# Windowed attention: one copy taken ahead of a masked score, one projection chunk and its rotation sooner, reciprocals behind rotations

## The chip, the cores and the metric

One Trainium2 chip, one of its cores. The time is that of the whole kernel on the device, in microseconds (us). An execution is one launch; the median of three launches is given. One further launch was profiled.

## What is computed

The program is a chain of four stages over 16 sequences of 512 tokens with 256 features: windowed attention, an int8 layer, a linear attention and a feed-forward layer, each followed by a layer norm. The change touches only the first stage, which the kernel does completely before the other three:

```
qkv = x @ w_qkv                                   # 16 heads of 64
q, k = l2norm(q) * q_scale, l2norm(k) * k_scale
bq = rotary(q * 8);  bk, bv = look_around(k, v)   # windows of 128; previous, own and next window
sim = where(mask, -big, einsum('bwid,bwjd->bwij', bq, bk))
out = einsum('bwij,bwjd->bwid', softmax(sim), bv)
x = layernorm(x + out @ w_out)
```

## The kernel before

All matrices are float32; projections are made of three products of high and low parts. The heads go in pairs, 8 pairs (p = 0 to 7) for each of 16 sequences, so 128 pairs. A sequence has four windows w = 0 to 3. Windows 0 and 3 have 256 keys, windows 1 and 2 have 384. In the code i is the number of a window counted over all pairs, n that of a pair, h the head in the pair (0 or 1).

Each engine runs its own program, written out by hand: for each pair two halves, u = 0 and u = 1 (`pe_half`, `act_half`, `dve_half`, `pool_half`). Work is done some way ahead. Half (p, u = 1) of pair n does three things side by side:

- it finishes windows 2 and 3 of pair n: TensorE transposes their softmax weights (`pe_transpose_weights`), ScalarE copies those of head 0 out of bank tp (`act_evacuate_weights`), VectorE those of head 1 (`dve_evacuate_weights`);
- it scores windows 0 and 1 of pair n+1: `pe_scores`, then on VectorE `dve_mask_max` (norm factor, mask, row maximum; the profile calls it CUSTOM_DVE_ANT_0), on ScalarE `act_exp` with the row sum, on VectorE `dve_reciprocals`, on GpSimd `pool_softmax` (scales the rows of both heads);
- it projects chunks 2 and 3 (of 128 tokens) of pair n+2: `pe_project` into banks pj, `act_project` on ScalarE (copy of v, square of q and k), `dve_rotate` on VectorE (two products, L510 and L511), `pool_rotate` on GpSimd (their sum).

Half (p+1, u = 0) then begins. On TensorE it is: `pe_values` of pair n (L331, weights times values, into bank qk), `pe_scores` of windows 2 and 3 of pair n+1 (L303), `pe_q_transpose` of pair n+2 (L278, into bank qk), and further on the transposes of windows 0 and 1 (L322), chunks 0 and 1 of the next projection (L267) and `pe_k_transpose` (L285). `pe_q_transpose` waits for `rot_pool`, that is for GpSimd's sum of chunk 3, and for `ot_act`, ScalarE's copy of the values' result (L445).

On GpSimd the order at this place is: softmax of window 0, softmax of window 1, rotation of chunk 2 (end of half u = 1), rotation of chunk 3, key norm (start of half u = 0). Its queue is in order, as are those of ScalarE and VectorE. `pool_softmax` waits for `rc_dve`, the reciprocal.

On VectorE half u = 1 ends: copy of window 2, `dve_mask_max` of window 1 head 1, reciprocal of window 0, copy of window 3, reciprocal of window 1, rotation of chunk 2. Half u = 0 starts: rotation of chunk 3, `dve_norms`, then the masked scores. On ScalarE half u = 1 ends with the exponential of window 1 head 1 and the projection of chunk 2, and half u = 0 starts with the projection of chunk 3.

A window is called spare when it is window 3 of a pair with p not 0 or 6. The transposes of head 1 of a spare window go to bank qk; those of other windows go to a score bank, sc.

Each sequence's layer norm is done while the next sequence runs: statistics of tokens in `dve_stats` (second half at the start of half (1,0)), `norm.rstd` on GpSimd at the end of half (1,0) (a power, L84, and a product, L86), `norm.apply` on ScalarE in half (2,0) ahead of `act_o_evacuate`.

The functions that the change touches:

Of the kernel before, what the change touches and what calls it, by code (L numbers as in the profile page):

```python
# [18 lines left out]
PAIRS = HEADS // 2  # L19
PW = 2 * DH  # L20
WS = 128
NW = S // WS
# [77 lines left out]
def run_attention(nc, io, mem, psum):  # L100
    SC, TP, PJ, QK = (psum['sc'], psum['tp'], psum['pj'], psum['qk'])

    def spare(i):
        pair, w = divmod(i, NW)
        return w == 3 and pair % PAIRS not in (0, 6)
# [14 lines left out]
    def span(w):  # L120
        lo, hi = (max(0, w - 1), min(NW - 1, w + 1))
        return lo, hi, (hi - lo + 1) * WS
# [200 lines left out]
        last.then_inc(g['t_pe'], 1)  # L323

    def pe_values(e, n, p):
        e.wait_ge(g['pt_act'], NW * n + NW)
        e.wait_ge(g['pt_dve'], NW * n + NW)
        for k in range(NW):
            lo, hi, width = span(k)
            for h in range(2):  # L330
                last = e.matmul(QK[rows(h), lo * WS:(hi + 1) * WS], v[p % 4][:, k, rows(h)], pt_keys(h, k),  # L331
                    start=k == 0, stop=k == NW - 1, skip_group_check=True)
        last.then_inc(g['pv_pe'], 1)
# [81 lines left out]
    def act_project(e, m, p, t):  # L415
        e.wait_ge(g['pj_pe'], TT * m + t + 1)
        e.activation(v[p % 4][:, t, :], PJ[t % 2][:, 2 * PW:3 * PW], ACT.Copy)
        e.activation(sq[:, t, :], PJ[t % 2][:, 0:2 * PW], ACT.Square).then_inc(g['sq_act'], 1)  # L418
# [11 lines left out]
    def act_exp(e, i, w, h):  # L430
        lo, hi, width = span(w)
        e.wait_ge(g['sm_dve'], 2 * i + h + 1)
        e.activation(ex[h][w][:, 0:width], sm[h][w % 2][:, 0:width], ACT.Exp, bias=nm[:, w, h:h + 1], scale=-1.0,  # L433
            accum_out=rs[:, w, h:h + 1]).then_inc(g['e_act'], 1)
# [16 lines left out]
    def act_half(e, at):  # L451
        n, p, u, i, w = (at.pair, at.p, at.u, at.window, at.w)
        ahead, next_i, next_w = (at.has_next(), at.next_window, at.next_w)
        if u == 0:
            if at.has_pair(1):
                act_project(e, n + 1, (p + 1) % PAIRS, 3)
            if at.at(2, 0) and not at.first:
                norm.apply(e, at.b - 1, mem['res'])
            if at.has_pair(-1):
                act_o_evacuate(e, n - 1, (p - 1) % PAIRS)  # L460
            if at.has_pair(1):
                act_norms(e, n + 1, (p + 1) % 2)
            if ahead:
                act_exp(e, next_i, next_w, 0)
            act_evacuate_weights(e, i, w)
            if ahead:
                act_exp(e, next_i, next_w, 1)
                act_exp(e, next_i + 1, next_w + 1, 0)
            if at.has_pair(2):
                act_project(e, n + 2, (p + 2) % PAIRS, w)  # L470
            if at.has_pair(1):
                act_k_evacuate(e, n + 1, (p + 1) % 2)
            act_evacuate_weights(e, i + 1, w + 1)
            if ahead:
                act_exp(e, next_i + 1, next_w + 1, 1)
        else:
            if at.has_pair(2):
                act_project(e, n + 2, (p + 2) % PAIRS, 1)
            if not at.last:
                if at.at(5, 1):  # L480
                    act_x(e, at.b + 1, 0)
                if at.at(6, 1):
                    act_x(e, at.b + 1, 1)
            act_evacuate_weights(e, i, w)
            if ahead:
                act_exp(e, next_i, next_w, 0)
                act_exp(e, next_i, next_w, 1)
                act_exp(e, next_i + 1, next_w + 1, 0)
            act_evacuate_weights(e, i + 1, w + 1)
            if ahead:  # L490
                act_exp(e, next_i + 1, next_w + 1, 1)
            if at.has_pair(2):
                act_project(e, n + 2, (p + 2) % PAIRS, w)
        if at.first and (at.at(0, 0) or at.at(2, 0)):
            act_weights_high(e, 3 + p // 2)
        if w1_piece(at) is not None:
            act_next_weights(e, w1_piece(at))
# [6 lines left out]
    def dve_rotate(e, m, t):  # L504
        e.wait_ge(g['sq_act'], TT * m + t + 1)
        if due(TT * m + t - 1):
            e.wait_ge(g['rot_pool'], TT * m + t - 1)
        heads = 'p (k h d) -> p k h d'
        qk = PJ[t % 2][:, 0:2 * PW].rearrange(heads, k=2, h=2)
        e.tensor_tensor(ra[:, t % 2, :].rearrange(heads, k=2, h=2), qk, rotary(t, 0), ALU.mult)  # L510
        last = e.tensor_tensor(rb[:, t % 2, :].rearrange(heads, k=2, h=2), qk, rotary(t, 1), ALU.mult)  # L511
        last.then_inc(g['rot_dve'], 1)

    def dve_norms(e, m):
        e.wait_ge(g['sq_act'], TT * m + TT)
        e.tensor_reduce(ss[:, 0, :], sq[:, :, :].rearrange('p t (h d) -> p (t h) d', d=DH), AX.X,
            ALU.add).then_inc(g['raw_dve'], 1)
        e.wait_ge(g['raw_dve'], m + 1)
        e.tensor_scalar(ss[:, 1, :], ss[:, 0, :], NORM_FLOOR ** 2, None, ALU.max).then_inc(g['ss_dve'], 1)
# [25 lines left out]
    def dve_residual(e, seq, k):  # L545
        e.wait_ge(g['op_pe'], 2 * seq + k + 1)
        if k == 0:
            e.wait_ge(g['x_keep'], 16 * (seq + 1))
            if due(seq):
                e.wait_ge(g['y_out'], 16 * seq)  # L550
        e.tensor_tensor(halves(mem['res'], k), QK[:, :], halves(mem['xres'], k), ALU.add).then_inc(g['op_dve'], 1)  # L551

    def dve_stats(e, seq, k):
        e.wait_ge(g['op_dve'], 2 * seq + k + 1)
        norm.stats(e, seq, mem['res'], (2 * k, 2 * k + 1))
# [7 lines left out]
    def dve_half(e, at):  # L563
        n, p, u, i, w = (at.pair, at.p, at.u, at.window, at.w)
        ahead, next_i, next_w, par = (at.has_next(), at.next_window, at.next_w, at.next_par)
        out = at.at(0, 1) and not at.first
        if u == 0 and at.has_pair(1):
            dve_rotate(e, n + 1, 3)
            dve_norms(e, n + 1)
        if u == 1 and at.has_pair(2):  # L570
            dve_rotate(e, n + 2, 1)
        if not at.first:
            if at.at(1, 0):
                dve_stats(e, at.b - 1, 1)
        if ahead:
            dve_mask_max(e, next_i, par, next_w, 0)
            dve_mask_max(e, next_i, par, next_w, 1)
        if not at.last:
            if at.at(5, 1):
                dve_x(e, at.b + 1, 0)  # L580
            if at.at(6, 1):
                dve_x(e, at.b + 1, 1)
        if u == 0 and at.has_pair(1):
            dve_q_evacuate(e, n + 1, (p + 1) % 2)
        if ahead:
            dve_mask_max(e, next_i + 1, par, next_w + 1, 0)
        if out:
            dve_residual(e, at.b - 1, 0)
        dve_evacuate_weights(e, i, w)
        if ahead:  # L590
            dve_mask_max(e, next_i + 1, par, next_w + 1, 1)
            dve_reciprocals(e, next_i, next_w)
        if out:
            dve_stats(e, at.b - 1, 0)
            dve_residual(e, at.b - 1, 1)
        dve_evacuate_weights(e, i + 1, w + 1)
        if ahead:
            dve_reciprocals(e, next_i + 1, next_w + 1)
        if at.has_pair(2):
            dve_rotate(e, n + 2, w)  # L600
        if at.first and (at.at(0, 1) or at.at(2, 1)):
            dve_weights_low(e, 3 + p // 2)
        if not at.first:
            for t, step in enumerate(((2, 1), (3, 0), (3, 1), (4, 0))):
                if at.at(*step):
                    dve_amax(e, at.b - 1, t)
# [27 lines left out]
    def pool_half(e, at):  # L634
        n, p, u, i, w = (at.pair, at.p, at.u, at.window, at.w)
        if u == 0 and at.has_pair(1):
            pool_rotate(e, n + 1, (p + 1) % 2, 3)
            pool_k_norm(e, n + 1, (p + 1) % 2)
        if u == 1 and at.has_pair(2):
            pool_rotate(e, n + 2, p % 2, 1)  # L640
        if at.has_next():
            pool_softmax(e, at.next_window, at.next_w)
            pool_softmax(e, at.next_window + 1, at.next_w + 1)
        if at.has_pair(2):
            pool_rotate(e, n + 2, p % 2, w)
        if at.at(1, 0) and not at.first:
            norm.rstd(e, at.b - 1)
        if at.first and (at.at(0, 1) or at.at(2, 1)):
            pool_weights_low(e, 3 + p // 2)
        if w1_piece(at) is not None:  # L650
            pool_next_weights(e, w1_piece(at))
# [1280 lines left out]
```

## Time and profile before

| | us |
|---|---|
| median of three launches (3098.9 to 3100.77) | 3100.35 |
| the profiled launch | 3097.64 |
| its span, first to last instruction | 3095.8 |
| TensorE busy | 2941.9 (95%) |
| VectorE busy | 2357.9 (76%) |
| ScalarE busy | 2162.1 (70%) |
| GpSimd busy | 1662.0 (54%) |

Busy times are of the whole span. Matmuls overlap their predecessors, so TensorE's busy share counts some waiting too: start times tell more than the share. In rows of the timeline the first number is the start in us from the start of the span, the second the length of the group; the bracket at the end gives the idle time before the group and what ended it. PE is TensorE, DVE VectorE, ACT ScalarE, POOL GpSimd.

### The profile page before, as it was taken

How to read it: one execution, taken by the hardware profiler on the slowest of the kernel's cores; microseconds unless marked ns; L12 is line 12 of the kernel's file. 1: busy time of each engine (PE TensorE's matmuls, PEld its weight loads, DVE VectorE, ACT ScalarE, POOL GpSimd, SP SyncE). 2: the span in 40 equal slices, each digit the busy share in tenths (PEclk: the TensorE clock that was granted, in tenths of full speed). 3: DMA queues.
4: the chain of work that ended last, by engine and by line, in shares of the span. 5: the costliest groups of instructions: out<-in, count | busy, mean ns of one | idle time of the engine just before them, and what ended most of it. 6: DMA issues, size and time to landing. Idle time of an engine off the chain costs nothing. (4 is left out here: it accounts for less than half of the span.)

```text
span 3095.8 us, 60269 instructions
## 1 busy us (share of the span) xinstructions
PE 2941.9 (95%) x20143; PEld 2332.4 (75%) x20143; DVE 2357.9 (76%) x6845; ACT 2162.1 (70%) x5670; POOL 1662.0 (54%) x2226
## 2 busy tenths in 40 slices
PE   7999999999999999999999996799999999999996
PEld 5777777777777777777777774578888888888885
DVE  6877877877877877877877875787777777777775
ACT  5666766766766766766766764577888888888884
POOL 5655655655655655655655654344555555555555
PEclk9999999999999999999999998899999999999998
DMA  2000000000000000000000002100000000000000
GB/s 84 8 15 22 8 15 22 8 15 22 8 15 17 13 15 15 15 15 15 15 15 15 8 21 64 47 15 8 15 15 15 21 20 16 15 15 15 8 15 21
DMA packets 51218, 57.50 MB, mean 19 GB/s; under 512 B 3008, under 2 KB 48592, under 8 KB 50912
## 3 DMA queue, kind: packets, MB, share of 16 engines
q1 hardware_dynamic: 47904, 50.67, 5.1%
q8 instruction: 164, 2.69, 0.4%
q10 hardware_dynamic: 3008, 2.98, 0.3%
q14 instruction: 142, 1.16, 0.1%
HBM read 36.86 MB, written 16.78 MB: 17 GB/s over the span
## 5 line engine op out<-in xcount | busy, mean ns | idle before, releaser
L627 POOL TENSOR_SCALAR a_ex<-a_ex,a_rc 128x384 f32<-128x384 f32 (+1 forms) x1024 | 533.8, 536 | 691.4 <-DVE a_rc L538 691.2
L433 ACT ACTIVATE a_ex<-a_sm,a_nm 128x384 f32<-128x384 f32 (+1 forms) x1024 | 572.0, 560 | 72.5 <-DVE a_nm L531 61.2
L531 DVE CUSTOM_DVE_ANT_0 a_sm<-sc,a_mask,a_rn 128x384 f32<-128x384 f32 (+1 forms) x1024 | 529.7, 543 | 6.3 <-PE sc L303 6.3
L439 ACT ACTIVATE a_pt<-tp 128x256 f32<-128x256 f32 (+1 forms) x512 | 220.1, 430 | 290.5 <-PE tp L322 290.5
L267 PE MATMUL pj<-a_whi,a_xhi 128*128 128x384 f32 x1024 | 390.3, 381 | 8.8 <-DVE a_wlo L187 5.8
L1695 POOL TENSOR_TENSOR b_alo<-b_ring,b_ahi 128x512 fp32r<-128x512 f32 x128 | 169.6, 1325 | 411.7 <-DVE b_ring L1524 388.0
L611 POOL TENSOR_TENSOR a_qr<-a_ra,a_rb 128x256 f32<-128x256 f32 x512 | 370.5, 739 | 11.2 <-DVE a_rb L511 8.4
L267 PE MATMUL pj<-a_whi,a_xlo 128*128 128x384 f32 x1024 | 347.4, 339 | 0.0
L267 PE MATMUL pj<-a_wlo,a_xhi 128*128 128x384 f32 x1024 | 346.3, 338 | 0.0
L331 PE MATMUL qk<-a_pt,a_v 128*64 128x384 f32 (+1 forms) x2048 | 303.9, 437 | 29.0 <-DVE a_pt L543 26.8
L303 PE MATMUL sc<-a_kT,a_qT 64*64 64x256 f32 (+1 forms) x4096 | 307.6, 415 | 1.6 <-DVE a_nm L531 0.9
L331 PEld LDWEIGHTS qk<-a_pt,a_v 128*64 128x64 f32 x2048 | 158.3, 136 | 156.3 <-issue 63.9
L543 DVE COPY a_pt<-sc 128x384 f32<-128x384 f32 (+1 forms) x416 | 209.7, 504 | 72.0 <-PE sc L322 65.9
L510 DVE TENSOR_TENSOR a_ra<-pj,a_rot 128x256 f32<-128x256 f32 x512 | 214.3, 419 | 39.9 <-ACT a_sq L418 39.7
L322 PE MATMUL tp<-s_ident,a_ex 128*128 128x128 f32 x1280 | 228.9, 277 | 3.2 <-ACT a_pt L439 1.3
L342 PE MATMUL qk<-a_wo,a_ot 128*128 128x256 f32 x1024 | 228.0, 381 | 1.5 <-DVE a_res L551 0.8
L303 PEld LDWEIGHTS sc<-a_kT,a_qT 64*64 64x64 f32 x4096 | 131.5, 132 | 129.0 <-issue 80.7
L342 PEld LDWEIGHTS qk<-a_wo,a_ot 128*128 128x128 f32 x1024 | 192.0, 190 | 34.5 <-issue 7.4
L1491 DVE SCALAR_TENSOR_TENSOR b_ring<-k,b_one_bk,b_ring 128x512 f32<-128x512 f32 x128 | 95.8, 749 | 153.1 <-ACT b_ring L1355 149.8
L511 DVE TENSOR_TENSOR a_rb<-pj,a_rot 128x256 f32<-128x256 f32 x512 | 211.6, 413 | 0.0
L267 PEld LDWEIGHTS pj<-a_whi,a_xhi 128*128 128x128 f32 x1024 | 194.5, 190 | 12.5 <-issue 6.3
L322 PE MATMUL sc<-s_ident,a_ex 128*128 128x128 f32 x1088 | 192.4, 278 | 8.3 <-DVE a_nm L531 4.9
(234 smaller groups left out, 7988.7 us busy)
## 6 DMA issues: line engine op xcount, KB each, us to landing
a_xres<-x SPq DMA_DIRECT2D x16, 512.0 KB, 3.8
y<-a_res SPq DMA_DIRECT2D x16, 512.0 KB, 2.9
b_y<-y SPq DMA_DIRECT2D x16, 512.0 KB, 3.8
a_xin<-x SPq DMA_DIRECT2D x15, 512.0 KB, 3.8
out<-b_y SPq DMA_DIRECT2D x15, 512.0 KB, 2.9
a_xin<-wqkv SPq DMA_DIRECT2D x8, 256.0 KB, 2.7
a_ot<-wqkv ACTq DMA_DIRECT2D x3, 384.0 KB, 9.8
a_stage<-wqkv SPq DMA_DIRECT2D x3, 384.0 KB, 12.3
```

The source lines that it names most:

```text
L267: last = e.matmul(PJ[t % 2][:, 0:3 * PW], a[:, c, t * P:(t + 1) * P], w[:, c, p * 3 * PW:(p + 1) * 3 * PW], start=c == 0 and k == 0, stop= ...
L303: last = e.matmul(SC[j][h][a * DH:(a + 1) * DH, first:first + wide], qT[par][rows(h), queries:queries + DH], kT[par][rows(h), lo * WS + fi ...
L322: last = e.transpose(tp_bank(h, i)[:, k * P:(k + 1) * P], ex[h][w][:, k * P:(k + 1) * P], ident[:, :])
L331: last = e.matmul(QK[rows(h), lo * WS:(hi + 1) * WS], v[p % 4][:, k, rows(h)], pt_keys(h, k), start=k == 0, stop=k == NW - 1, skip_group_c ...
L342: last = e.matmul(QK[:, t * DIM:(t + 1) * DIM], ot[:, c, (2 * k + t) * P:(2 * k + t + 1) * P], wo[:, c, :], start=c == 0, stop=c == HC - 1)
L433: e.activation(ex[h][w][:, 0:width], sm[h][w % 2][:, 0:width], ACT.Exp, bias=nm[:, w, h:h + 1], scale=-1.0, accum_out=rs[:, w, h:h + 1]).t ...
L439: e.activation(pt_window(0, w), blocks(TP, w), ACT.Copy).then_inc(g['pt_act'], 1)
L510: e.tensor_tensor(ra[:, t % 2, :].rearrange(heads, k=2, h=2), qk, rotary(t, 0), ALU.mult)
L511: last = e.tensor_tensor(rb[:, t % 2, :].rearrange(heads, k=2, h=2), qk, rotary(t, 1), ALU.mult)
L531: e.tensor_tensor_reduce(out=sm[h][w % 2][:, 0:width], in0=SC[w % 2][h][:, 0:width], in1=mem['mask'][:, off:off + width], scale=rn[:, par, ...
L611: e.tensor_tensor(qr[par][:, t, :].rearrange(half, h=4, s=2), ra[:, t % 2, :].rearrange(half, h=4, s=2), rb[:, t % 2, :].rearrange(half, h ...
L627: e.tensor_scalar(row, row, 0.0, rc[:, w, h:h + 1], ALU.add, ALU.mult).then_inc(g['exn_pool'], 1)
```

## The change

In `pe_values` the wait for all four windows' copies is split: key windows 0 and 1 start after three windows' copies (where window 3 is spare, VectorE's copies of all four are still awaited), key windows 2 and 3 after all four. In halves u = 1 ScalarE projects chunk 2 right after the first exponential. In halves u = 1 with a spare window, VectorE copies window 3 and rotates chunk 2 ahead of the last `dve_mask_max`, and the reciprocal of window 1 moves into the next half, behind the rotation of chunk 3. In halves u = 0 the last reciprocal goes behind the rotation of chunk 0. The second part of `dve_stats` moves from the start of half (1,0) to its end, and `norm.rstd` from half (1,0) to half (1,1).

```diff
     def pe_values(e, n, p):
-        e.wait_ge(g['pt_act'], NW * n + NW)
-        e.wait_ge(g['pt_dve'], NW * n + NW)
         for k in range(NW):
             lo, hi, width = span(k)
+            if k in (0, 2):
+                e.wait_ge(g['pt_act'], NW * n + NW - 1 + k // 2)
+                e.wait_ge(g['pt_dve'], NW * n + (NW if k or spare(NW * n + NW - 1) else NW - 1))
...
             act_evacuate_weights(e, i, w)
             if ahead:
                 act_exp(e, next_i, next_w, 0)
+            if at.has_pair(2):
+                act_project(e, n + 2, (p + 2) % PAIRS, w)
+            if ahead:
                 act_exp(e, next_i, next_w, 1)
                 act_exp(e, next_i + 1, next_w + 1, 0)
             act_evacuate_weights(e, i + 1, w + 1)
             if ahead:
                 act_exp(e, next_i + 1, next_w + 1, 1)
-            if at.has_pair(2):
-                act_project(e, n + 2, (p + 2) % PAIRS, w)
...
         if u == 0 and at.has_pair(1):
             dve_rotate(e, n + 1, 3)
+        if u == 0 and i and spare(i - 1):
+            dve_reciprocals(e, i + 1, w + 1)
+        if u == 0 and at.has_pair(1):
             dve_norms(e, n + 1)
         if u == 1 and at.has_pair(2):
             dve_rotate(e, n + 2, 1)
-        if not at.first:
-            if at.at(1, 0):
-                dve_stats(e, at.b - 1, 1)
...
         dve_evacuate_weights(e, i, w)
-        if ahead:
+        if ahead and u == 1 and spare(i + 1):
+            dve_evacuate_weights(e, i + 1, w + 1)
+            if at.has_pair(2):
+                dve_rotate(e, n + 2, w)
             dve_mask_max(e, next_i + 1, par, next_w + 1, 1)
             dve_reciprocals(e, next_i, next_w)
-        if out:
-            dve_stats(e, at.b - 1, 0)
-            dve_residual(e, at.b - 1, 1)
-        dve_evacuate_weights(e, i + 1, w + 1)
-        if ahead:
-            dve_reciprocals(e, next_i + 1, next_w + 1)
-        if at.has_pair(2):
-            dve_rotate(e, n + 2, w)
+        else:
+            if ahead:
+                dve_mask_max(e, next_i + 1, par, next_w + 1, 1)
+                dve_reciprocals(e, next_i, next_w)
+            if out:
+                dve_stats(e, at.b - 1, 0)
+                dve_residual(e, at.b - 1, 1)
+            dve_evacuate_weights(e, i + 1, w + 1)
+            if u == 0 and at.has_pair(2):
+                dve_rotate(e, n + 2, w)
+            if ahead:
+                dve_reciprocals(e, next_i + 1, next_w + 1)
+            if u == 1 and at.has_pair(2):
+                dve_rotate(e, n + 2, w)
+        if at.at(1, 0) and not at.first:
+            dve_stats(e, at.b - 1, 1)
...
-        if at.at(1, 0) and not at.first:
+        if at.at(1, 1) and not at.first:
             norm.rstd(e, at.b - 1)
```

## Rows read from the trace of the kernel before

**Rows 1.** Timeline of PE, half (7,1) and the next: start, length, engine, line.
```profile
957.19 1.20 PE L303 MATMUL sc<-a_kT,a_qT 64*64 64x256 f32 x16
...
959.76 0.49 PE L322 MATMUL sc<-s_ident,a_ex 128*128 128x128 f32 x3
...
961.92 2.38 PE L331 MATMUL qk<-a_pt,a_v 128*64 128x256 f32 x16 [0.19 <-DVE a_pt L543]
964.23 1.20 PE L303 MATMUL sc<-a_kT,a_qT 64*64 64x320 f32 x16
965.36 0.66 PE L278 MATMUL qk<-s_ident,a_qr 128*128 128x128 f32 x4
...
969.61 0.66 PE L303 MATMUL sc<-a_kT,a_qT 64*64 64x256 f32 x8
```

**Rows 2.** Timeline of DVE, same stretch.
```profile
960.29 0.56 DVE L543 COPY a_pt<-sc 128x384 f32<-128x384 f32 x1 [0.21 <-PE sc L322]
960.76 0.61 DVE L531 CUSTOM_DVE_ANT_0 a_sm<-sc,a_mask,a_rn 128x384 f32<-128x384 f32 x1
...
961.29 0.16 DVE L538 RECIPROCAL a_rc<-a_rs 128x2 f32<-128x2 f32 x1
961.37 0.41 DVE L543 COPY a_pt<-qk 128x256 f32<-128x256 f32 x1
...
962.59 0.42 DVE L510 TENSOR_TENSOR a_ra<-pj,a_rot 128x256 f32<-128x256 f32 x1 [0.27 <-ACT a_sq L418]
...
963.26 0.41 DVE L510 TENSOR_TENSOR a_ra<-pj,a_rot 128x256 f32<-128x256 f32 x1
```

**Rows 3.** Timeline of ACT, same stretch.
```profile
961.41 0.61 ACT L433 ACTIVATE a_ex<-a_sm,a_nm 128x384 f32<-128x384 f32 x1 [0.17 <-DVE a_nm L531]
...
962.18 0.37 ACT L418 ACTIVATE a_sq<-pj 128x256 f32<-128x256 f32 x1
```

**Rows 4.** Timeline of POOL, same stretch.
```profile
961.56 2.07 POOL L627 TENSOR_SCALAR a_ex<-a_ex,a_rc 128x256 f32<-128x256 f32 x4 [1.72 <-DVE a_rc L538]
963.59 1.42 POOL L611 TENSOR_TENSOR a_qr<-a_ra,a_rb 128x256 f32<-128x256 f32 x2
```

**Rows 5.** Timeline of PE, half (4,1) and the next half's query transposes.
```profile
917.85 1.20 PE L303 MATMUL sc<-a_kT,a_qT 64*64 64x256 f32 x16
...
926.47 0.66 PE L278 MATMUL qk<-s_ident,a_qr 128*128 128x128 f32 x4
```

**Rows 6.** Timeline of PE, half (1,1) and the next half's query transposes.
```profile
879.50 1.20 PE L303 MATMUL sc<-a_kT,a_qT 64*64 64x256 f32 x16
...
888.03 0.63 PE L278 MATMUL qk<-s_ident,a_qr 128*128 128x128 f32 x4 [0.15 <-ACT a_ot L445]
```

**Rows 7.** Timeline of POOL, end of half (1,0) and start of (1,1).
```profile
881.85 1.02 POOL L84 TENSOR_TENSOR a_ln_rs<-a_ln_ve,a_half 128x4 f32<-128x4 f32 x1
...
883.10 0.74 POOL L611 TENSOR_TENSOR a_qr<-a_ra,a_rb 128x256 f32<-128x256 f32 x1
```

**Rows 8.** Timeline of ACT, half (2,0).
```profile
885.32 2.08 ACT L92 ACTIVATE a_res<-a_res,a_ln_shift,a_ln_rs 128x256 f32<-128x256 f32 x4
```

**Rows 9.** Timeline of PE in the first sequence: the query transposes that waited.
```profile
33.46 0.66 PE L278 MATMUL qk<-s_ident,a_qr 128*128 128x128 f32 x4 [2.32 <-POOL a_qr L611]
...
39.28 0.93 PE L303 MATMUL sc<-a_kT,a_qT 64*64 64x256 f32 x12
...
50.32 0.66 PE L278 MATMUL qk<-s_ident,a_qr 128*128 128x128 f32 x4 [2.01 <-POOL a_qr L611]
...
80.02 0.66 PE L278 MATMUL qk<-s_ident,a_qr 128*128 128x128 f32 x4 [2.10 <-POOL a_qr L611]
```

**Rows 10.** Windows: length, busy us (count) of each engine, PEclk, DMA share, GB/s.
```profile
34.10:37.50 3.40, 3.40 (x16) 3.30 (x14) 2.50 (x9) 2.79 (x10) 1.05 (x1) 0.50 0.02 5
51.10:54.50 3.40, 3.40 (x15) 3.30 (x15) 1.91 (x7) 2.19 (x8) 0.36 (x1) 0.51 0.00 0
81.50:85.00 3.50, 3.50 (x33) 2.95 (x35) 2.50 (x10) 3.29 (x12) 1.62 (x4) 1.00 0.00 0
```

## Prediction

> **What bounds the kernel now.** I read the page first: TensorE is the fullest engine, and the stage that the change touches is the first of four. Then I read the timeline of TensorE over one sequence by start times, because overlapping matmuls hide waits in a busy share. Nearly every step from one matmul to the next is as short as it can be for its shapes. The exceptions are small: in most pairs the values (L331) start late, waiting for VectorE's copy of window 3; the bracket says 0.19 us in the pair shown [rows 1]. So TensorE bounds the stage, and the other engines matter only where a result that it awaits comes late. The timelines of the three others over the same stretch tell how much room each result has. The one with least room is the query transposes (L278): TensorE reaches them at 965.36 [rows 1], and GpSimd's sums of chunks 2 and 3 end at 963.59 + 1.42 = 965.01 [rows 4]. That is 0.35 us of slack, at the end of a queue that starts with the softmax scaling of windows 0 and 1.
>
> **The chain to the query transposes, before.** Last masked score 960.76, its exponential 961.41 [rows 2, 3], GpSimd busy without a gap from 961.56 to 965.01, with the softmax of both windows first and both rotations after [rows 4]. I call the start of the half's scores T0 = 957.19; the transposes come at T0 + 8.17, the next half's scores at 969.61, 4.25 us after them [rows 1].
>
> **The same chain after, step by step.** VectorE's queue now holds the copies of windows 2 and 3, the rotation of chunk 2, and only then the last masked score.
> 1. Copy of window 2: it waits for TensorE's transposes at present (idle 0.21) and starts at 960.29; they aren't earlier now. It takes 0.47 to the next start [rows 2].
> 2. Copy of window 3 (narrow): 0.41 long [rows 2], of which some 0.06 overlaps the next instruction, as every VectorE group here starts a little before its predecessor's end; 0.35. At 961.11 window 3 is copied. TensorE could start the values sooner by the bracket's 0.19; I take 0.25, since overlapping starts hide a little of a wait, so 961.67 instead of 961.92, and this copy doesn't hold it up any more. That is the gain, and it is right.
> 3. Rotation of chunk 2: 963.26 - 962.59 = 0.67 [rows 2]. Its input is ready, since ScalarE now projects chunk 2 two exponentials sooner. Ends 961.78.
> 4. Last masked score starts 961.78 instead of 960.76: 1.02 us later.
> 5. Its exponential 0.65 after the score's start (960.76 to 961.41), as before [rows 2, 3]: 962.43. ScalarE then goes straight on to chunk 3 of the projection. Before, chunk 2 stood between; its square starts 0.77 after the exponential [rows 3]. I use that 0.77 for chunk 3's: 963.20.
> 6. Rotation of chunk 3 starts 0.41 after the square (962.18 to 962.59) [rows 2, 3]: 963.61. It takes 0.67: 964.28.
> 7. Only now comes the reciprocal of window 1, which was free to run since about 963.1. GpSimd starts 0.27 after a reciprocal (961.29 to 961.56) [rows 2, 4]: 964.55.
> 8. Softmax of window 1: all four scalings take 963.59 - 961.56 = 2.03 [rows 4], by width 384/640 of that, 1.22: 965.77.
> 9. Rotations of chunks 2 and 3 stand behind it in GpSimd's queue, though chunk 2's products have been there for 4 us: 1.42 [rows 4], 967.19; transposes at 967.24, T0 + 10.05.
>
> So the query transposes come 10.05 - 8.17 = 1.88 us later, although TensorE is through with values and scores 0.25 sooner. What follows them is TensorE's own work, 4.25 us to the next T0, and the next half u = 1 starts from the same state, because step 1 hangs on TensorE. The delay repeats in each pair.
>
> **The sum over a sequence.** Halves like (7,1): pairs 7 and 2, and I take pair 5 (which also splits the next input) as the same: 3 x 1.88 = 5.64. Pairs 3 and 4 lose 8.62 already (917.85 to 926.47 [rows 5]), a wait that goes with the earlier rotation of chunk 0: 2 x (10.05 - 8.62) = 2.86. Pair 6 keeps VectorE's order, but there ScalarE now waits, with two exponentials and a copy queued behind it, for a projection that TensorE does only after window 3's first transposes; both reciprocals and GpSimd hang on these exponentials. No row prices it; it lies between 0 (slack hides it) and 1.88 (the chain above), and I take 1.0, nearer the middle.
>
> Pair 1 is the dear one. The rstd moves from GpSimd's idle stretch to the place between rotations of chunks 2 and 3, and takes 883.10 - 881.85 = 1.25 [rows 7]. Worse, `norm.apply` on ScalarE waits for it, and behind it are queued the copy of the values' result and the norms. Rotation 2 ends at T0 + 10.05 - 0.05 - 0.71 = T0 + 9.29; rstd until 10.54; apply at 10.59; from the apply's start to the transposes it is 888.03 - 885.32 = 2.71 as now [rows 6, 8]: T0 + 13.30. Before: 888.03 - 879.50 = 8.53 [rows 6]. That is 4.77. Moving `dve_stats` gives TensorE something back in half (1,0), whose key transposes wait for VectorE, and costs most of it again at the next masked scores: no row separates these; between a gain of 0.8 and a loss of 0.6 I take 0.2 gained. Pair 1: 4.6. Pair 0 gets 0 (a gain of at most 0.2).
>
> Per sequence 5.64 + 2.86 + 1.0 + 4.6 = 14.1. Fourteen full ones: 197. The first has no norm to do (pair 1 as pair 7, 11.4), the last nothing after pair 5 (11.2). Together 220 us.
>
> The split wait of `pe_values` itself costs nothing: key windows 2 and 3 come half of 2.3 us after the first (961.92 to 964.23 [rows 1]), and ScalarE's copy, one projection later than before, is there by then. If it were not, TensorE would wait some tenths, in time that it now waits anyway at the transposes.
>
> **The clock.** TensorE will stand still from the end of the scores, 963.98 + 1.20 = 965.18, to 967.24: 2.0 us in each of 80 pairs and over 5 us in 15 (pair 1). The trace has three such stalls at the same instruction: 2.32, 2.01 and 2.10 us [rows 9]. After two of them the granted clock was 0.50 (the 1.2 GHz level), after the third 1.00 [rows 10]. The first of them took 39.28 - 33.46 = 5.82 from transposes to next scores [rows 9] against 4.25 [rows 1]: 1.57 us for a fall. I take a fall after every second of the 80, between none and all: 63 us, and one in each pair 1: 24 us.
>
> The Trainium skill, page "TensorE: Matmul & The Clock Gate", section "HAM oscillation — how this bites in real kernels", describes how a loop that waits between bursts of matmuls finds the clock throttled again each time. Taken to the letter for every pair here it gives 149 us where I take 87; the two stalls of three agree with it, the third speaks against "each time".
>
> **Sum.** The profiled launch took 3097.64, the median 3100.35, 2.7 more. 220 + 87 = 307; 3097.64 + 307 + 2.7 = 3407, which I round to 3405 us.
>
> **The rivals.**
> - *Stalls without the clock* (chance 0.17): the delay is as above but the clock stays at 1.00, as after the third stall; 3100 + 220 = 3320. For it: full work on both sides of the stall.
> - *A fall after every stall* (0.12), the skill's rule taken to the letter: 3320 + 95 x 1.57 = 3469.
> - *Only the sequence boundary hurts* (0.07): the rotations turn out to leave room in ordinary pairs, and pair 1's rstd and apply alone are late: 3100 + 15 x 4.6 = 3169. Against it: 0.35 us of slack and 2.2 us more in the chain.
> - *Faster* (0.08): GpSimd's chain stays hidden, so that TensorE keeps what it gains at the values, 0.19 to 0.25 in a pair (128 x 0.25 = 32 us), and some waits of masked scores and key transposes on top, 20 us: about 3050. It decides itself at step 7: window 1's reciprocal would have to run by some 962.7, 1.6 us before my 964.28, for instance if ScalarE had chunk 3 done before the last exponential. The order of its queue speaks against that.
> - *No change* (0.03): the gains and pair 1's loss cancel, which needs ordinary pairs to lose nothing.
>
> My forecast, with falls after part of the stalls, has 0.53. Faster and slower are counted from 0.2%, about what measurement of this kernel can tell from no change: faster 0.08, same 0.03, slower 0.89. The range goes from somewhat under the case without the clock (3290) to the case of all falls (3470).
>
> **What would show it.** In the trace after: TensorE's L278 idle some 2 us with GpSimd's L611 named, in pairs 1 to 5 and 7, over 5 us once a sequence with ScalarE's L445 named; no idle at L331 before the values; GpSimd idle between the softmaxes of window 0 and 1; stretches of clock 0.50 all through the first stage; the other stages unchanged. I am wrong if the reciprocal of window 1 doesn't end up behind a rotation that waits for ScalarE, or if TensorE does other work during that time.

## The result

The changed kernel takes 3375.5 us (median of 6 launches, 3373.4 to 3379.4) against 3099.6 for the kernel before in the same session: ratio 1.089, 95% interval 1.0876 to 1.0904. The forecast was 3405 us, slower. (In two of the experiments below one launch of four took far longer, 5817 and 10133 us, for a reason that nothing here shows; their times are medians of the other three.) The profiled launch has a span of 3377.6 us against 3095.8, 281.8 more. The last matmul of the attention stage ends at 2192.4 instead of 1914.2, so 278 of these 282 us are in that stage.

The page of the kernel after (span, and busy time, share and number of instructions by engine) has TensorE 89% busy instead of 95%, with the same 20143 matmuls:

```profile
span 3377.6 us, 60397 instructions
PE 3012.0 (89%) x20143; PEld 2398.0 (71%) x20143; DVE 2364.3 (70%) x6845; ACT 2194.2 (65%) x5670; POOL 1661.0 (49%) x2226
```

TensorE's waits, from 200 to 1800 us (us in total, times, longest):

```profile
PE qk L278 <- POOL a_qr L624: 124.6, 72, 2.0
PE qk L278 <- ACT a_ot L446: 63.8, 12, 5.3
PE sc L322 <- DVE a_nm L533: 7.2, 11, 0.7
```

Before, in the same stretch:

```profile
PE qk L331 <- DVE a_pt L543: 22.8, 82, 0.5
...
PE qk L278 <- ACT a_ot L445: 1.5, 10, 0.2
```

The largest wait, that of the values (L331) for VectorE's copy, is gone: where rows 1 have a bracket of 0.19 at the values, there is none now. In its place stand 72 waits of the query transposes (L278) for GpSimd's rotation and, once a sequence, one of 5.3 us for ScalarE's copy of the values' result.

Half (7,1) after, TensorE; it answers to [rows 1]:

```profile
1092.71 1.20 PE L303 MATMUL sc<-a_kT,a_qT 64*64 64x256 f32 x16
...
1095.28 0.49 PE L322 MATMUL sc<-s_ident,a_ex 128*128 128x128 f32 x3
...
1097.19 2.38 PE L332 MATMUL qk<-a_pt,a_v 128*64 128x256 f32 x16
1099.49 1.20 PE L303 MATMUL sc<-a_kT,a_qT 64*64 64x320 f32 x16
1102.62 0.66 PE L278 MATMUL qk<-s_ident,a_qr 128*128 128x128 f32 x4 [1.92 <-POOL a_qr L624]
...
1106.88 1.20 PE L303 MATMUL sc<-a_kT,a_qT 64*64 64x256 f32 x16
```

With T0 = 1092.71 the values start at T0 + 4.48 (before 4.73) and the transposes at T0 + 9.91 (before 8.17). The next scores follow 4.26 later (before 4.25). VectorE, which answers to [rows 2]:

```profile
1095.81 0.56 DVE L545 COPY a_pt<-sc 128x384 f32<-128x384 f32 x1 [0.24 <-PE sc L322]
1096.28 0.41 DVE L545 COPY a_pt<-qk 128x256 f32<-128x256 f32 x1
1096.61 0.42 DVE L512 TENSOR_TENSOR a_ra<-pj,a_rot 128x256 f32<-128x256 f32 x1
...
1097.27 0.61 DVE L533 CUSTOM_DVE_ANT_0 a_sm<-sc,a_mask,a_rn 128x384 f32<-128x384 f32 x1
...
1097.81 0.16 DVE L540 RECIPROCAL a_rc<-a_rs 128x2 f32<-128x2 f32 x1
1099.10 0.42 DVE L512 TENSOR_TENSOR a_ra<-pj,a_rot 128x256 f32<-128x256 f32 x1 [1.13 <-ACT a_sq L419]
...
1099.78 0.16 DVE L540 RECIPROCAL a_rc<-a_rs 128x2 f32<-128x2 f32 x1
```

ScalarE [rows 3] and GpSimd [rows 4]:

```profile
1097.01 0.38 ACT L440 ACTIVATE a_pt<-tp 128x256 f32<-128x256 f32 x1
1097.93 0.62 ACT L434 ACTIVATE a_ex<-a_sm,a_nm 128x384 f32<-128x384 f32 x1 [0.54 <-DVE a_nm L533]
...
1098.70 0.37 ACT L419 ACTIVATE a_sq<-pj 128x256 f32<-128x256 f32 x1
```

```profile
1098.07 0.94 POOL L640 TENSOR_SCALAR a_ex<-a_ex,a_rc 128x256 f32<-128x256 f32 x2 [2.45 <-DVE a_rc L540]
1100.03 1.15 POOL L640 TENSOR_SCALAR a_ex<-a_ex,a_rc 128x384 f32<-128x384 f32 x2 [1.02 <-DVE a_rc L540]
1101.15 1.42 POOL L624 TENSOR_TENSOR a_qr<-a_ra,a_rb 128x256 f32<-128x256 f32 x2
```

Read in this order it is the chain of the forecast: the score starts at 1097.27, behind a copy and a rotation; exponential 1097.93; square of chunk 3 1098.70; its rotation 1099.10, for which VectorE sat idle 1.13 us, while the reciprocal stood behind it; reciprocal 1099.78; softmax of window 1 at 1100.03; and both rotations on GpSimd only at 1101.15, though the products of chunk 2 were complete by 1097.4. GpSimd idles 2.45 and 1.02 us ahead of the two softmaxes. The values start at 1097.19 while ScalarE's copy of window 3 (L440) runs until 1097.39: so their gain needs the split wait as well as VectorE's sooner copy. The mended kernel with VectorE's old order, below, has the split wait without the sooner copy, and its values start at T0 + 4.73 again; no run has the sooner copy alone.

The sequence boundary, half (1,1) and (2,0), on TensorE [rows 6], GpSimd [rows 7] and ScalarE [rows 8]:

```profile
863.22 1.20 PE L303 MATMUL sc<-a_kT,a_qT 64*64 64x256 f32 x16
...
866.61 0.52 PE L322 MATMUL sc<-s_ident,a_ex 128*128 128x128 f32 x3 [0.66 <-DVE a_nm L533]
...
877.37 1.09 PE L278 MATMUL qk<-s_ident,a_qr 128*128 128x128 f32 x4 [5.30 <-ACT a_ot L446]
```

```profile
872.65 0.73 POOL L624 TENSOR_TENSOR a_qr<-a_ra,a_rb 128x256 f32<-128x256 f32 x1
873.34 1.02 POOL L84 TENSOR_TENSOR a_ln_rs<-a_ln_ve,a_half 128x4 f32<-128x4 f32 x1
874.43 0.20 POOL L86 TENSOR_TENSOR a_ln_shift<-a_ln_minus,a_ln_rs 128x4 f32<-128x4 f32 x1
874.59 0.72 POOL L624 TENSOR_TENSOR a_qr<-a_ra,a_rb 128x256 f32<-128x256 f32 x1
```

```profile
874.67 2.08 ACT L92 ACTIVATE a_res<-a_res,a_ln_shift,a_ln_rs 128x256 f32<-128x256 f32 x4 [4.09 <-POOL a_ln_shift L86]
876.65 0.58 ACT L446 ACTIVATE a_ot<-qk 128x512 f32<-128x512 f32 x1
```

ScalarE stands 4.09 us in front of the apply. Its copy of the values' result is queued behind, and the transposes behind that: T0 + 14.15, before T0 + 8.53. At the bracket of 0.66, ahead of the transposes of softmax weights, TensorE pays for the statistics, which VectorE now does ahead of this half's masked scores.

The same two distances for all pairs, medians over the sequences (15 in pairs 6 and 7, 16 in the others), each from the start times in the timeline of TensorE (those at full clock where there are any, so that only pair 1 after has the clock's cost in it; "mended" is an experiment below):

| pair | T0 to query transposes: before | after | mended | then to the next T0: before | after | mended |
|---|---|---|---|---|---|---|
| 0 | 21.94 | 21.78 | 21.78 | 5.22 | 4.26 | 5.21 |
| 1 | 8.52 | 14.15 | 8.29 | 4.22 | 6.52 | 4.23 |
| 2 | 8.16 | 9.91 | 7.91 | 4.40 | 4.27 | 4.26 |
| 3 | 8.62 | 9.90 | 7.91 | 4.41 | 4.26 | 4.26 |
| 4 | 8.62 | 9.90 | 7.91 | 4.25 | 4.27 | 4.26 |
| 5 | 8.73 | 10.40 | 8.34 | 4.25 | 4.25 | 4.26 |
| 6 | 9.23 | 9.94 | 9.15 | 4.26 | 4.26 | 4.25 |
| 7 | 8.17 | 9.90 | 7.91 | 4.26 | 4.26 | 4.26 |

The granted clock of a stretch behind a stall of 1.92 us in another sequence's pair 7, and behind one of 5.3 us (columns as in [rows 10]):

```profile
967.60:971.00 3.40, 3.40 (x15) 3.31 (x15) 1.81 (x7) 2.34 (x8) 0.39 (x2) 0.50 0.00 0
875.40:878.80 3.40, 1.43 (x7) 1.46 (x8) 0.30 (x1) 2.75 (x8) 1.05 (x1) 0.51 0.33 112
875.40:882.20 6.80, 4.83 (x20) 4.76 (x21) 1.99 (x7) 4.85 (x16) 1.05 (x1) 0.50 0.23 77
```

I call such a stretch at 0.50 a fall of the clock. Where it fell in an ordinary pair (2 to 5 and 7), the way from the transposes to the next scores took 5.83 us instead of 4.26; in the pair 1 shown the low clock lasted until 882.2, and the way took 6.52. It fell after 4 of 16 stalls in pair 2, none in pair 3, 9 of 16 in pair 4, 8 of 16 in pair 5, 8 of 15 in pair 7 and all 16 in pair 1. Between the first and the last sequence the falls of pairs 4 and 7 come in every second sequence, and those of pair 5 in the others.

These stalls aren't all of one length. In the first sequence that of pair 1 is 1.92 us and that of pair 2 3.83, in the last those of pairs 4 and 5 are 3.7. Sorted by length, the clock fell after 27 of 77 stalls of 1.9 to 2.0 us, after all 3 of 3.7 to 3.8 and all 15 of 5.3.

### The profile page after: what moved, and what is told of

Its sections match the earlier page's. It is cut to its first block and busy times, and to the rows that moved or that the text cites. A ratio compares the mean times of both kernels' runs of the same rounds, so it can differ in the third digit from the quotient of the medians.

```text
span 3377.6 us, 60397 instructions
## 1 busy us (share of the span) xinstructions
PE 3012.0 (89%) x20143; PEld 2398.0 (71%) x20143; DVE 2364.3 (70%) x6845; ACT 2194.2 (65%) x5670; POOL 1661.0 (49%) x2226
## 5 line engine op out<-in xcount | busy, mean ns | idle before, releaser
L440 ACT ACTIVATE a_pt<-tp 128x256 f32<-128x256 f32 (+1 forms) x512 | 223.2, 436 | 386.4 <-PE tp L322 385.6
L267 PE MATMUL pj<-a_whi,a_xhi 128*128 128x384 f32 x1024 | 405.3, 396 | 8.3 <-DVE a_wlo L187 5.0
L267 PE MATMUL pj<-a_whi,a_xlo 128*128 128x384 f32 x1024 | 361.6, 353 | 0.0
L267 PE MATMUL pj<-a_wlo,a_xhi 128*128 128x384 f32 x1024 | 360.1, 352 | 0.0
L278 PE MATMUL qk<-s_ident,a_qr 128*128 128x128 f32 x512 | 91.3, 305 | 255.2 <-POOL a_qr L624 175.5
L278 PEld LDWEIGHTS qk<-s_ident,a_qr 128*128 128x128 f32 x512 | 58.7, 150 | 311.5 <-POOL a_qr L624 219.6
L322 PE MATMUL tp<-s_ident,a_ex 128*128 128x128 f32 x1280 | 244.2, 292 | 8.4 <-ACT a_pt L440 7.8
L332 PEld LDWEIGHTS qk<-a_pt,a_v 128*64 128x64 f32 x2048 | 137.1, 137 | 143.1 <-issue 120.7
L322 PE MATMUL sc<-s_ident,a_ex 128*128 128x128 f32 x1088 | 204.7, 292 | 9.9 <-DVE a_nm L533 9.8
```

The source lines that it names most:

```text
L267: last = e.matmul(PJ[t % 2][:, 0:3 * PW], a[:, c, t * P:(t + 1) * P], w[:, c, p * 3 * PW:(p + 1) * 3 * PW], start=c == 0 and k == 0, stop= ...
L322: last = e.transpose(tp_bank(h, i)[:, k * P:(k + 1) * P], ex[h][w][:, k * P:(k + 1) * P], ident[:, :])
L440: e.activation(pt_window(0, w), blocks(TP, w), ACT.Copy).then_inc(g['pt_act'], 1)
```

## The experiments

Each was timed against the kernel before on the same chip. The theory: the query transposes are the end of one serial chain (last masked score, exponential, square of chunk 3, rotation of chunk 3, reciprocal, softmax of window 1, two rotations on GpSimd), and at the sequence boundary of a longer one through rstd and apply; stalls cost a second time through the clock.

**Reciprocal ahead of the rotation of chunk 3.** On the changed kernel:

```diff
         if u == 0 and at.has_pair(1):
-            dve_rotate(e, n + 1, 3)
         if u == 0 and i and spare(i - 1):
             dve_reciprocals(e, i + 1, w + 1)
         if u == 0 and at.has_pair(1):
+            dve_rotate(e, n + 1, 3)
             dve_norms(e, n + 1)
```

> The changed kernel with one edit: window 1's deferred reciprocal stands ahead of the rotation of chunk 3, not behind it. Theory (GpSimd's queue holds both rotations behind the softmax of window 1, which waits for this reciprocal): the reciprocal runs when the last exponential is done instead of about 1.1 us later, so the query transposes come about 1.0 us sooner after T0 (8.9 instead of 9.9), the stall before them shrinks from 1.92 to about 0.95 us in each of 80 pairs and by 1.0 in pair 1, and the clock stops falling in ordinary pairs (about 32 falls of 1.57 us): 3375 - 95 - 50 = 3230 us. Rival (the rotation of chunk 2 ahead of the last masked score alone makes the stall, the reciprocal's place is covered): query transposes stay at T0 + 9.9 and the time at 3375 us.

Measured: 3240.8 us (ratio 1.0453, 1.0438 to 1.0469), transposes at T0 + 8.85. In ordinary pairs the clock falls three times only, once in the first sequence and twice in the last, after stalls of 3.4, 2.2 and 2.1 us, and after none of the stalls of at most 1.0 us.

```profile
PE qk L278 <- POOL a_qr L623: 66.8, 78, 1.0
PE qk L278 <- ACT a_ot L446: 51.1, 12, 4.3
```

(the same waits, same stretch). The longest stalls went from 2.0 to 1.0 and from 5.3 to 4.3: the reciprocal's place is 1.05 us of the chain and was not covered. 135 us of the 276 hang on the order of two neighbouring instructions; summed over the pairs of the two traces, some 98 are the sooner transposes and 37 the clock. The rival is out.

**Last masked score ahead of the rotation of chunk 2**, reciprocal still deferred. On the changed kernel:

```diff
             dve_evacuate_weights(e, i + 1, w + 1)
-            if at.has_pair(2):
-                dve_rotate(e, n + 2, w)
             dve_mask_max(e, next_i + 1, par, next_w + 1, 1)
             dve_reciprocals(e, next_i, next_w)
+            if at.has_pair(2):
+                dve_rotate(e, n + 2, w)
```

> The changed kernel with the rotation of chunk 2 behind the last masked score and the first reciprocal again; the copy of window 3 stays ahead of the score, the second reciprocal stays deferred. Theory (the chain from the last masked score is serial down to the query transposes, so each part of the delay counts by its own length): the transposes come 0.67 us sooner, at T0 + 9.23 instead of 9.90; the stall of 1.25 us no longer brings the clock down. 3375 - 95 x 0.67 - 50 = 3262 us. Rival (the deferral alone makes the stall and the rotation's place is covered): T0 + 9.9 and 3375 us.

Measured: 3270.1 us (1.0545, 1.053 to 1.0559), transposes at T0 + 9.25. The rotation counts by its 0.65 us, so the two parts of the delay add up, as in a serial chain: with the copy's 0.33 they make 2.03, and the chain's end moved from T0 + 7.82 (before) to T0 + 9.86, by 2.04.

**Layer norm at its old places.** On the changed kernel:

```diff
+        if not at.first:
+            if at.at(1, 0):
+                dve_stats(e, at.b - 1, 1)
         if ahead:
             dve_mask_max(e, next_i, par, next_w, 0)
...
-        if at.at(1, 0) and not at.first:
-            dve_stats(e, at.b - 1, 1)
...
-        if at.at(1, 1) and not at.first:
+        if at.at(1, 0) and not at.first:
             norm.rstd(e, at.b - 1)
```

> The changed kernel with the layer norm's statistics and rstd at their old places (start and end of half (1,0)). Theory (rstd between the two rotations delays the apply and all that stands behind it on ScalarE): the stalls of 5.3 us in pair 1 become stalls of about 1.9 us, 15 falls of the clock go with them, and the key transposes of half (1,0) wait 0.9 us again: 15 x (3.4 + 2.3 - 0.9) = 72 us less, 3303 us. Rival (pair 1's long stall hides other late work, so that little comes back): 3355 us or more.

Measured: 3299.5 us (1.0643, 1.0626 to 1.0661), 76 us less than the changed kernel; pair 1 at T0 + 9.89, like its neighbours, and the key transposes of half (1,0) wait again (T0 of the next half 5.21 after the transposes, not 4.26). The ordinary stalls are as long as in the changed kernel (1.91 us, in the last sequence 3.7 in pairs 4 and 5), but the clock now falls after all 31 in pairs 4 and 7 and after none in pair 3: the length of such a stall alone doesn't decide it.

**Only the layer norm moved.** On the kernel before:

```diff
-        if not at.first:
-            if at.at(1, 0):
-                dve_stats(e, at.b - 1, 1)
...
+        if at.at(1, 0) and not at.first:
+            dve_stats(e, at.b - 1, 1)
...
-        if at.at(1, 0) and not at.first:
+        if at.at(1, 1) and not at.first:
             norm.rstd(e, at.b - 1)
```

> The kernel before with only the statistics and rstd moved as in the change. Theory: pair 1 alone loses. Rstd's 1.25 us and the apply behind it put the query transposes of half (2,0) about 2.7 us later, half (1,0) gives back about 0.9 and half (1,1) loses most of that at its first masked scores, and the clock falls in each of these 15 stalls of over 3 us: 15 x (2.6 + 1.57) = 63 us more, 3163 us. Rival (the move is harmless by itself and hurts only behind the delayed rotations): 3100 us, or some 13 us under it, by the 0.9 us that the key transposes no longer wait.

Measured: 3155.8 us (1.0182, 1.016 to 1.0205; launches of 3151 to 3164). The waits of the values are as before; new is

```profile
PE qk L278 <- ACT a_ot L445: 37.4, 13, 2.9
```

The longest is 2.9 us, not 5.3: here rstd has a shorter chain in front of it. The clock fell after 12 of the 15. This part alone costs some 56 us; undone in the changed kernel it gave 76.

**The stall filled.** On the changed kernel, transposes that nothing reads:

```diff
         if u == 0:
+            if at.has_pair(1) and n and spare(NW * n - 1):
+                for k in range(17):
+                    e.transpose(TP[:, (k % 4) * P:(k % 4 + 1) * P], ident[:, :], ident[:, :])
             if at.has_pair(1):
                 pe_q_transpose(e, n, n + 1, (p + 1) % 2)
```

> The changed kernel with 17 further transposes of the identity matrix into the free bank tp, ahead of each query transposes that follow a pair with a spare window. They take 17 x 0.109 = 1.85 us of TensorE and fall in its stall; nothing reads them. Theory (the stall costs a second time through the clock): the query transposes stay at T0 + 9.9, but the half-clock stretches behind the stalls of 1.92 us are gone, 32 x 1.57 = 50 us less, 3325 us; those behind pair 1's long stalls may stay. Rival (the slower sections aren't caused by the stall but by something else in these pairs): as many half-clock stretches as before and 3375 us.

Measured: 3314.5 us (1.0685, 1.0665 to 1.0706), 61 us less with 1615 matmuls more. The filler lies in the stall:

```profile
911.41 1.20 PE L303 MATMUL sc<-a_kT,a_qT 64*64 64x320 f32 x16
912.54 2.08 PE L368 MATMUL tp<-s_ident 128*128 128x128 f32 x17
914.60 0.66 PE L278 MATMUL qk<-s_ident,a_qr 128*128 128x128 f32 x4
```

The transposes stay at T0 + 9.91 and the clock no longer falls in pairs 2 to 7; it still falls in 13 of the 15 pairs 1 in which a stall, now of 3.3 us, is left. So the falls come from the stalls. 29 falls in pairs 2 to 7 at 1.57 us are 46 us; in pair 1 the ways to the next T0 are 15 us shorter in sum (where the clock fell, 5.81 instead of 6.52). Together that is the measured 61.

**GpSimd rotates ahead of the softmax of window 1.** On the changed kernel:

```diff
         if u == 0 and at.has_pair(1):
             pool_rotate(e, n + 1, (p + 1) % 2, 3)
+        if u == 0 and i:
+            pool_softmax(e, i + 1, 1)
+        if u == 0 and at.has_pair(1):
             pool_k_norm(e, n + 1, (p + 1) % 2)
...
         if at.has_next():
             pool_softmax(e, at.next_window, at.next_w)
-            pool_softmax(e, at.next_window + 1, at.next_w + 1)
+            if u == 0:
+                pool_softmax(e, at.next_window + 1, at.next_w + 1)
```

> The changed kernel with another order on GpSimd: both rotations ahead of the softmax of window 1, which moves into the next half behind the rotation of chunk 3. VectorE's order, the deferred reciprocal included, stays. Theory (the reciprocal hurts only because two rotations are queued behind its softmax): the query transposes of ordinary pairs come at T0 + 7.95, where TensorE itself arrives, and no stall is left there; in pair 1 rstd and apply still stand ahead, T0 + 11.1, with a fall of the clock. 3375 - 156 - 50 - 46 = about 3120 us, between 3100 and 3130. Rival (VectorE's products of chunk 3 are themselves too late, behind ScalarE's last exponential): a stall of 1 us or more is left in ordinary pairs and the time stays over 3200 us.

Measured: 3177.0 us (1.0245, 1.0227 to 1.0264). The transposes come at T0 + 8.01, as expected, but the time is 47 us over the expected range. Two things that I hadn't counted: from the transposes to the next T0 it takes 4.63 instead of 4.26 us, because the key transposes now wait for VectorE's copy of the query transposes, which is queued behind the rotation of chunk 3, the norms and two masked scores; and in pair 1 the clock fell after 13 of 15 stalls of 3.2 us, and the way from the transposes to the next T0 took 7.05 us there, 1.25 us more than one fall costs elsewhere.

**The same with rstd sooner**, behind the rotation of chunk 1 in half (1,1):

```diff
         if u == 1 and at.has_pair(2):
             pool_rotate(e, n + 2, p % 2, 1)
+        if at.at(1, 1) and not at.first:
+            norm.rstd(e, at.b - 1)
...
-        if at.at(1, 1) and not at.first:
-            norm.rstd(e, at.b - 1)
```

> As the kernel with the new GpSimd order, and rstd at the start of half (1,1), behind the rotation of chunk 1, where GpSimd waits for the first reciprocal anyway. Theory: nothing of the delay is left, TensorE keeps what the change gives it at the values (0.25 us in a pair, more in pairs 3 and 4) and at the key transposes of half (1,0) (0.9 us a sequence): about 2.5 to 3.5 us a sequence less than the kernel before, 3050 to 3060 us. Rival (the late softmax of window 1 now holds up its transposes, or the norms the key transposes): a new wait of TensorE at L322 or L285 and 3100 us or more.

Measured: 3107.3 us (1.0030, 1.0018 to 1.0042): the first theory's gain isn't there, the rival is right. TensorE's waits:

```profile
PE qk L285 <- DVE a_qT L525: 14.9, 84, 0.2
PE qk L278 <- ACT a_ot L446: 14.5, 13, 1.1
PE sc L322 <- DVE a_nm L533: 8.5, 13, 0.7
```

The 84 small waits at the key transposes are the new bound. The bracket shows at most 0.2 us; by start times each costs 0.37. Pair 1 loses too: T0 + 9.95, before 8.52, of which half (1,0) gives back 0.96.

**The kernel before with the GpSimd order alone** (the two edits of `pool_half` shown above, nothing else).

> The kernel before with the new GpSimd order alone. Theory: there the query transposes wait for nothing of GpSimd's and TensorE bounds the pair, so a sooner rotation brings nothing: 3100 us, within 0.3%. Rival (GpSimd's queue was a bound already before): 10 us or more less.

Measured: 3103.8 us (1.0013, 1.0004 to 1.0022), a tenth of a per cent slower. Nothing to gain there: the query transposes of pairs 2, 3, 4 and 7 come when they came before (T0 + 8.17 and 8.62), since they didn't wait for GpSimd.

**The mended kernel.** GpSimd's new order, the score ahead of the rotation, the layer norm at its old places, and for pair 6

```diff
-            if at.has_pair(2):
+            if at.has_pair(2) and p != 6:
                 act_project(e, n + 2, (p + 2) % PAIRS, w)
...
             if ahead:
                 act_exp(e, next_i + 1, next_w + 1, 1)
+            if at.has_pair(2) and p == 6:
+                act_project(e, n + 2, (p + 2) % PAIRS, w)
```

> The changed kernel with four things mended: GpSimd rotates ahead of the softmax of window 1; the last masked score and the first reciprocal stand ahead of the rotation of chunk 2 again (the copy of window 3 stays first); the layer norm's statistics and rstd at their old places; in half (6,1) ScalarE projects chunk 2 last, as before. Theory: the chain of the last masked score is 0.67 us shorter, so VectorE's norms no longer hold up the key transposes (0.35 us in a pair in the kernel with the GpSimd order alone), the query transposes come at T0 + 7.92, and pair 6 loses nothing: some 3 us a sequence less than before, 3050 to 3060 us. Rival (VectorE or ScalarE is the next bound at another place and takes it back): 3090 us or more.

Measured: 3047.6 us, ratio 0.9832 (0.9819 to 0.9846). This beats both kernels. The row of pair 7 in the table: 7.91 to the transposes, the 0.26 us that the values gained and nothing given back. Most of the gain lies elsewhere, though: pairs 3, 4 and 5 gain 0.86, 0.70 and 0.38 us, 31 of the 50 us between the two profiled launches. What TensorE still waits for:

```profile
PE qk L285 <- DVE a_qT L527: 9.0, 14, 0.6
PE tp L322 <- ACT a_pt L440: 4.7, 14, 0.3
```

**The mended kernel with VectorE's old order in halves u = 1:**

```diff
-        if u == 0 and i and spare(i - 1):
-            dve_reciprocals(e, i + 1, w + 1)
...
-        if ahead and u == 1 and spare(i + 1):
+        if False:
```

> As the mended kernel, but with VectorE's old order in halves u = 1 (last masked score, first reciprocal, copy of window 3, second reciprocal, rotation of chunk 2). It tells what the copy ahead of the score is worth. Theory: the copy then ends about 0.1 us after TensorE could start the values, and chunk 3's rotation may come a little sooner: within 10 us of the mended kernel, 3055 to 3070 us. Rival (the copy ahead is the heart of the gain): 3090 us or more.

Measured: 3076.7 us (0.9923, 0.9911 to 0.9935), 29 us over the mended kernel, more than I expected and less than the rival says. The values start at T0 + 4.73 again, and the query transposes come 0.26 us later in pairs 2 to 4 and 7 and 0.32 in pair 5 (in pair 1 at the same time, 8.29); pairs 2 and 3 also take 0.15 more to the next T0. That is 1.7 us a sequence, some 26 us in all; the profiled launches differ by 25. VectorE's order, the copy of window 3 ahead of the score above all, is worth half of the gain or a little more; the edit also moves the second reciprocal. The rest stays: pairs 3 and 4 are at T0 + 8.17, not 8.62. GpSimd's order alone left them at 8.62 in the kernel before, so it comes from the other parts of the change, or from the orders together; no run separates these.

**The mended kernel with the layer norm moved:** statistics at the end of half (1,0), as in the changed kernel, and rstd at the start of half (1,1), by the same lines as in the kernel with rstd sooner.

> As the mended kernel, but with the statistics at the end of half (1,0) and rstd at the start of half (1,1). Theory: half (1,0) gains 0.95 us at the key transposes, and half (1,1) loses 0.8 us at its masked scores and some at the query transposes, since ScalarE's apply follows the late work: 0 to 1 us a sequence more than the mended kernel, 0 to 15 us. Rival (with the shorter chain the move pays): 10 us less than the mended kernel.

Measured: 3045.8 us (0.9825, 0.9812 to 0.9839), the same as the mended kernel as far as the intervals tell. Half (1,0) gains 0.96 us and pair 1 loses 1.0 (T0 + 9.29 instead of 8.29).

## Why the prediction was right, and where its terms were off

**The gain at the values** was forecast as 0.25 us in a pair like (7,1): measured 4.73 to 4.47. Right, and the change does what it is for. In pairs 3 and 4 the values gain more, from 5.19 to 4.47; the transposes' wait swallows that too.

**The chain in ordinary pairs.** Forecast T0 + 10.05, measured 9.91; each step came within 0.1 us. The largest miss is step 8, the softmax of window 1, taken as 1.22 and measured 1.12 to the next start. The misses of the other steps are of 0.02 or less. Pairs 2 and 7 lose 1.74 us (forecast 1.88), 3 and 4 1.28 (1.43), 5 1.67 (1.88), 6 0.71 (1.0, a value chosen between bounds). That the reciprocal's place and the rotation's are parts of one serial chain was shown by taking them out one at a time: 1.05 and 0.65 us.

**Pair 1.** Forecast 4.77 us, minus 0.2: measured 14.15 - 8.52 = 5.63, and half (1,0) gives back 0.96, and pair 0 0.16. Net 4.5 against 4.6. Of the 5.63 some 0.86 are the statistics ahead of this half's first masked scores (the values start at T0 + 5.33, in other pairs at 4.47); without them it is 4.77, as forecast. What moving the statistics gives and costs, 0.96 and 0.86, nearly cancels; the 0.2 in the forecast was a choice between bounds.

**The delays together.** Per sequence 1.75 - 0.13 + 1.28 - 0.15 + 1.28 + 1.67 + 0.71 + 1.73 + 5.63 - 1.12 = 12.7 us from the table, against 14.1. All of its terms were forecast too high; and not forecast at all was that pairs 2 and 3 take 0.13 and 0.15 us less from the transposes to the next T0.

**The clock.** Forecast 40 falls after ordinary stalls and 15 in pair 1, 87 us. Counted: 29 after ordinary stalls, 46 us at 1.57; and pair 1, where the way to the next T0 takes 2.3 us more in the median instead of 1.57, about 35 us. Together some 80. That this is near 87 is partly luck: the ordinary stalls cost 17 us less than forecast and pair 1 11 more. That half of the stalls brings a fall was the weakest term, read from three stalls; it was 29 of 79, very unevenly over the pairs. The Trainium skill ("TensorE: Matmul & The Clock Gate", section "HAM oscillation — how this bites in real kernels") describes a loop whose waits of some 3 to 5 us between bursts of matmuls throttle the clock each time. The 15 stalls of 5.3 us agree with it. The prediction applied it to stalls of 2 us, which are shorter than the waits described there; after those of 1.9 to 2.0 us the clock fell in 27 of 77 cases, so neither always nor never. What makes the difference between pair 3 (none) and pair 4 (9 of 16), whose stalls are equal but for the last sequence's, is open: the kernel with the layer norm at its old places shows only that it changes with the order of the work around.

The sum of these, 12.7 x 15.5 + 80 = 277 (the first and the last sequence lose less than a full one), is the 278 us of the stage. I forecast 307: 23 too much in the chain and 7 in the clock.

**The rivals.** "Only the sequence boundary hurts" is out by the kernel with the layer norm at its old places, which still loses 6.4%; "stalls without the clock" and "a fall after every stall" are out by the counts, and the filled stall shows that the falls cost what was forecast for one.

**What the prediction left out** was that the same idea could pay. It treated GpSimd's queue as given; with another order there, and with VectorE's score and first reciprocal ahead of the rotation, the copy's gain is kept. Whether VectorE's order alone would do (reciprocal and score both ahead of the rotations, GpSimd as it was) was not run. An estimate from the two single steps, 9.91 - 1.05 - 0.65 = 8.21 against 7.91, says that 0.3 us a pair would be left.

## What to carry to other kernels

When an instruction is put behind another in an in-order queue, follow the result that it makes through every queue of the other engines to the next instruction of the bounding engine: here 0.1 us of work, a reciprocal, carried two unrelated rotations and a matmul with it, and cost half of the 276 us, about a quarter of that half through the clock. Before an order is changed to remove a small wait, read how much slack the next result has (0.35 us here); where there is little, reorder the consuming queue first, by the time at which its consumers need each item. Do the sum by start times: of a short wait of TensorE the bracket showed only a part (0.2 of 0.37 us).

## What the runs showed of the hardware

Stalls of TensorE of 1.9 to 2.0 us at the query transposes, with dense work on both sides, brought the granted clock to 0.50 (the 1.2 GHz level) in 27 of 77 cases in the changed kernel, at 1.57 us each; in the kernel with the layer norm at its old places the same stalls did so in every case in pairs 4 and 7 and in none in pair 3. Stalls of at most 1.0 and 1.4 us, in ordinary pairs of the kernels with the reciprocal or the score first, brought none. Stalls of 2.9 us (only the layer norm moved), 3.2 us (GpSimd's new order) and 3.3 us (the stall filled), all in pair 1, brought a fall in 12, 13 and 13 of 15 cases, and those of 4.3, 4.7 and 5.3 us in all 45. Filling a stall with matmuls that nobody reads made the kernel 61 us faster, without starting any needed work sooner.
